# Graph attention kernel: the node stage's five transfers take four consecutive nodes on a partition

## The chip, the cores and the metric

One core of one Trainium2 chip runs the whole program in one launch. The metric is device microseconds of one execution of that program. The kernel before takes 4809.48 us, the median of 3 runs (4803.77 to 4822.28 us).

## What is computed

The graph has 50000 nodes and 50000 edges, sorted by their target node. Node rows are 256 floats wide. Two rounds are computed, each closed by a residual sum and a layer norm:

```python
edge_index = jnp.stack([src, dst])
x = _layernorm(x + gat(x, edge_index, edge_attr_32, lin_W, att_src, att_dst, ...))
x = _layernorm(x + edge_mlp(x, edge_attr_128, src, dst, W0, b0, W1, b1, W2, b2, Wg))
```

The first round is graph attention with 4 heads of 64 and a self loop on every node: per target node a softmax over its edges' logits, then the weighted sum of the sources' projected rows. The second round takes for every edge the rows of its source and target, h = tanh([x_src, x_dst] @ W0 + b0), two further layers, a gate from the edge's 128 attributes, and the mean of the results over the edges of the same source.

## The kernel before

**Stages.** The program is a series of blocks; at the end of each all engines meet. In order of time: weights and keys (to 26 us), a histogram of the target keys (to about 220 us), a rank stage that also projects x and stores it as the table XP (to 1022 us), a message stage in sorted order that writes a table CT of running sums (to 1568 us), a short block that repairs sums across tiles, the **node stage** (1622 to 2698 us), the edge stage (to about 4505 us) and the last layer norm. Edges and nodes are handled in 98 groups of 512, that is G = 4 tiles of P = 128.

**Two orders of the 512 rows of a group.** The helper `tiles(a, g)` (L103) puts row p of tile t on partition p, at place t: a partition holds four rows that lie 128 rows apart in memory, and each is its own run of bytes. The helper `nodes(a, g)` (L107) puts rows 4p to 4p + 3 on partition p: one run four times as long. The rank stage already loads x (L157 in `load_nodes`) and stores XP (L688) by `nodes`.

**The node stage** (L1297 to L1545) makes, for each group g, the row of the first round: the node's last running sum from CT, its own projected row from XP, and x.
- SP (L1329) waits for `n_row` of group g - 2, then loads `n_xp` from XP (528 KB, rows of 1056 bytes) and `n_x` from x (512 KB, rows of 1024 bytes, through `load_rows`, L148).
- POOL (L1336) raises the variance of group g to the power -0.5, then copies four columns of `lastd` into `n_last` (L1340) and issues four indirect gathers of 128 rows of CT for group g + 2 (L1344). Nothing of POOL is queued behind them but the next group's power.
- VectorE (L1428) works in a fixed order: statistics of group g (L1401 to L1408), `exponents` of group g + 1 (L1371 to L1376, of which L1374 needs the gathers), the low halves of group g - 1 (L1419), `shift` (L1413), `row` of group g + 1 (L1381 to L1395). The last operation of `row` releases the loads of group g + 3.
- ScalarE norms the rows (L1492), stores them to `out` (L1497), evacuates the products (L1516) and stores the tables PA (L1521, rows of 1632 bytes) and PB (L1522, rows of 1624 bytes).
- TensorE transposes the normed rows and multiplies them by both halves of W0, each as three products of rounded parts (L1468), 48 matmuls of 406 columns a group.

**Tables that depend on the order.** `lastd` holds for each node the row of CT with its last sum. It is made in the histogram stage in the order of `nodes` (`lastf`, L572) and turned into the order of `tiles` at the end of the rank stage: 16 matmuls with selection matrices `place` (L751 to L755), which POOL fills in the histogram stage (L482 to L488). `rcn` is the reciprocal count of each source; it is counted in the rank stage from two digits of the source key, `LO[1]` and `HI[1]` (L323 to L329), low 7 bits and the rest, which is the order of `tiles`. TensorE's last matmul of that stage (L757) turns the counts of signs into differences, and L819 and L820 make the reciprocal.

Of the kernel before, what the change touches and what calls it, by code (L numbers as in the profile page):

```python
# [21 lines left out]
P = 128  # L22
G = 4
# [33 lines left out]
def gnn_kernel(nc, x, src, dst, e128, e32, lin_W, att_src, att_dst, lin_edge_W, att_edge, bias,  # L57
# [105 lines left out]
    with top:  # L163
# [52 lines left out]
        ki = [alloc(srt, f"key_digit{q}", [P, NT], i32) for q in range(5)]  # L216
# [5 lines left out]
        KEYS_READY = 13  # L222
        ph = ExitStack()
        with ph:
# [6 lines left out]
            with nc.Block(no_gpsimd_drain=True) as block:  # L231
# [67 lines left out]
                def _(dve):  # L299
# [23 lines left out]
                    c.did(nc.vector.tensor_scalar(ki[1][:], KI[:, 1, 0:NT], P - 1, None, ALU.bitwise_and))  # L323
                    c.did(nc.vector.tensor_scalar(ki[3][:], KI[:, 1, 0:NT], 7, None, ALU.arith_shift_right))
# [4 lines left out]
                    c.did(nc.vector.tensor_scalar(HI[1][:], ki[3][:], -0.5, None, ALU.add))  # L329
# [38 lines left out]
        with srt:  # L368
# [4 lines left out]
            place = alloc(srt, "place", [P, G * G, P])  # L373
# [66 lines left out]
            with ph:  # L440
# [15 lines left out]
                with nc.Block(no_gpsimd_drain=True) as block:  # L456
# [15 lines left out]
                    @block.gpsimd  # L472
                    def _(pool):
                        nc.gpsimd.memset(far[:], -BIG).then_inc(h_pad, 1)
                        pool.wait_ge(h_pad, 3)
                        nc.gpsimd.memset(far[:].rearrange("p (r w) -> p r w", w=DW)[:, :, DW - 1:DW], 0.0).then_inc(h_pad, 1)
                        nc.gpsimd.memset(steps[:], 0.0).then_inc(h_pad, 1)
                        for n, (base, fill) in enumerate(((0, 1.0), (1, -1.0), (1 - P, 1.0))):
                            pool.wait_ge(h_pad, 5 + n)
                            nc.gpsimd.affine_select(out=steps[:], in_=steps[:], compare_op=ALU.not_equal, fill=fill,  # L480
                                                    base=base, pattern=[[-1, P]], channel_multiplier=1).then_inc(h_pad, 1)
                        nc.gpsimd.memset(place[:], 0.0).then_inc(h_pad, 1)  # L482
                        pool.wait_ge(h_pad, 9)
                        for r in range(G):
                            for k in range(G):
                                nc.gpsimd.affine_select(out=place[:, r * G + k, :], in_=place[:, r * G + k, :],
                                                        compare_op=ALU.not_equal, fill=1.0, base=k - r * P,
                                                        pattern=[[-1, P]], channel_multiplier=G).then_inc(h_pad, 1)  # L488
# [111 lines left out]
            with ph:  # L600
# [3 lines left out]
                LB = B[3]  # L604
# [13 lines left out]
                with nc.Block(no_gpsimd_drain=True) as block:  # L618
# [81 lines left out]
                    def _(pe):  # L700
# [46 lines left out]
                        pe.wait_ge(r_ot, GROUPS)  # L747
                        pe.wait_ge(h_pad, 9 + G * G)
                        by_quad = lastf[:].rearrange("p (g t) -> p g t", t=G)
                        by_tile = LB[:, 0:NT].rearrange("p (g t) -> p g t", t=G)  # L750
# [9 lines left out]
                    def _(dve):  # L760
# [65 lines left out]
        with ph:  # L826
# [36 lines left out]
            with nc.Block(no_gpsimd_drain=True) as block:  # L863
# [34 lines left out]
                def _(dve):  # L898
# [5 lines left out]
                    dve.wait_ge(h_pad, 10 + G * G)  # L904
# [393 lines left out]
        with ph:  # L1298
# [27 lines left out]
            with nc.Block(no_gpsimd_drain=True) as block:  # L1326
                @block.sync
                def _(sp):
                    def body(g, s, i, last):  # L1329
                        need(sp, n_row, g - 1)  # L1330
                        sp.dma_start(xpn[s][:], tiles(XP, g)).then_inc(n_ld[s], 16)
                        load_rows(sp, xin[s], x, g, last, n_x[s])
# [32 lines left out]
                def _(dve):  # L1365
# [12 lines left out]
                    def row(g, s, i, last):  # L1378
# [12 lines left out]
                        dve.wait_ge(n_x[s], 16 * (i + 1) + 16 * last)  # L1391
# [36 lines left out]
                    def body(g, s, i, last):  # L1428
# [8 lines left out]
                        if not late(g, 1):  # L1437
                            row(g + 1, 1 - s, i if s == 0 else i + 1, late(g, 2))
# [3 lines left out]
                    row(0, 0, 0, False)  # L1442
# [40 lines left out]
                def _(act):  # L1483
# [4 lines left out]
                    def norm(g, s, i, last):  # L1488
# [10 lines left out]
                        act.dma_start(tiles(out, g, TAIL_TILES), x1[s][:, 0:TAIL_TILES, :]).then_inc(x1_st[s], 16)  # L1499
                        act.dma_start(out[N - TAIL_ROWS:N, :], x1[s][0:TAIL_ROWS, TAIL_TILES, :]).then_inc(x1_st[s], 16)  # L1500
# [40 lines left out]
                    act.wait_ge(x1_st[0], 16 * PAIRS)  # L1541
                    act.wait_ge(x1_st[1], 16 * PAIRS + 16)
                    for s in range(2):
                        act.wait_ge(pa_st[s], 16 * PAIRS)
# [505 lines left out]
```

## Time and profile before

| | us |
|---|---|
| median of 3 runs | 4809.48 |
| lowest, highest | 4803.77, 4822.28 |
| span of the profiled execution | 4813.1 |
| node stage, first DMA issue to the next stage's | 1621.8 to 2698.0 |

| engine | busy us | share of the span |
|---|---|---|
| TensorE | 3972.5 | 83% |
| VectorE | 3729.6 | 77% |
| ScalarE | 3089.0 | 64% |
| GpSimd | 2981.9 | 62% |

HBM is read for 567.01 MB and written for 431.82 MB. Of 717533 DMA packets 591298 are under 2 KB. Three queues carry them: q0 is GpSimd's indirect transfers (software), q1 is issued by SyncE and q10 by ScalarE (hardware). Their packets took 30.3%, 19.8% and 21.6% of the 16 engines' time over the whole span.

How to read it: the shares are means over stages that differ. The stage of the change has to be read by itself, in windows of time. A group of 512 nodes in it is one period of every engine, and the question is which wait in a period ends last. The time in which a queue's packets were moved is given as a share of 16 DMA engines; a share times 16 times the length of the window, divided by the bytes, is the engine time of a megabyte. Packets of one engine may overlap, so a share can be a little over 100%.

### The profile page before, as it was taken

The numbers are of one execution on the slowest core, as the hardware profiler recorded it, in microseconds if no ns is written. First come the engines' busy times: TensorE is split into PE (matmuls) and PEld (weight loads), VectorE is DVE, ScalarE is ACT, GpSimd is POOL, SyncE is SP. The second block draws the span as 40 slices with busy tenths as digits, with TensorE's granted clock in tenths as the row PEclk, the third lists the DMA queues.
The fourth block names the chain that finished last, engine by engine and source line by source line (L and its number), as shares of the span: only waits on it lengthen the run. The fifth ranks groups of instructions, "written<-read, shape, count | busy, mean of one in ns | idle before, by whom it ended". The sixth has DMA issues, their size and how long they took to land. (4 is left out here: it accounts for less than half of the span.)

```text
span 4813.1 us, 84225 instructions
## 1 busy us (share of the span) xinstructions
PE 3972.5 (83%) x23546; PEld 3291.7 (68%) x23546; DVE 3729.6 (77%) x11631; ACT 3089.0 (64%) x7157; POOL 2981.9 (62%) x2765
## 2 busy tenths in 40 slices
PE   5899999977777499999999799999999999999200
PEld 3466666655555399999999687777788778777200
DVE  6899999978888699898989476666666666666564
ACT  6866666645555266666666477776777767776575
POOL 1055556567777355555555377777777778777322
PEclk9999999988999699999999899999999999999655
DMA  4255554558666499999999577766767766766696
GB/s 105 51 171 169 168 171 167 169 148 212 199 201 202 151 360 364 349 365 353 365 359 362 175 152 154 153 149 153 152 150 153 154 152 149 153 150 152 218 394 261
DMA packets 717533, 1002.80 MB, mean 208 GB/s; under 512 B 186862, under 2 KB 591298, under 8 KB 704182
## 3 DMA queue, kind: packets, MB, share of 16 engines
q0 software_dynamic: 160768, 323.45, 30.3%
q10 hardware_dynamic: 245565, 375.01, 21.6%
q1 hardware_dynamic: 310861, 300.30, 19.8%
q8 instruction: 154, 2.52, 0.2%
q14 instruction: 185, 1.52, 0.1%
HBM read 567.01 MB, written 431.82 MB: 208 GB/s over the span
## 5 line engine op out<-in xcount | busy, mean ns | idle before, releaser
L1468 PE MATMUL bank<-w0r,n_x1T 128*128 128x406 f32 x4704 | 903.3, 351 | 41.1 <-ACT n_pa L1516 38.9
L1468 PEld LDWEIGHTS bank<-w0r,n_x1T 128*128 128x128 f32 x4704 | 868.0, 189 | 65.6 <-ACT n_pa L1516 63.4
L1612 POOL DMA_INDIRECT out_x<-u_sums,u_row x392 | 635.8, 1622 | 144.4 <-issue 117.1
L1664 PE MATMUL bank<-u_h,w1r 128*108 128x512 f32 (+1 forms) x2646 | 692.4, 407 | 0.0
L635 POOL DMA_INDIRECT DS<-payload,rank_int x392 | 378.2, 965 | 477.0 <-DVE rank_int L810 386.5
L1344 POOL DMA_INDIRECT n_cg<-CT,n_last x392 | 452.0, 1153 | 174.4 <-issue 95.2
L1664 PEld LDWEIGHTS bank<-u_h,w1r 128*108 128x108 f32 (+1 forms) x2646 | 444.5, 175 | 129.8
L1595 POOL DMA_INDIRECT u_pa<-PA,key_int x392 | 388.2, 990 | 167.2 <-issue 120.1
L891 POOL DMA_INDIRECT xg<-XP,ds x392 | 412.4, 1052 | 125.9 <-issue 121.3
L1664 PE MATMUL bank<-w2r,u_h 108*128 108x256 f32 x3528 | 479.2, 280 | 0.0
L427 PE MATMUL bank<-wst,xT 128*128 128x264 f32 x1568 | 421.3, 391 | 51.0 <-DVE xps L436 50.8
L1595 POOL DMA_INDIRECT u_pb<-PB,key_int x392 | 384.2, 980 | 119.5 <-issue 119.5
L1664 PEld LDWEIGHTS bank<-w2r,u_h 108*128 108x128 f32 x3528 | 444.1, 188 | 0.1
L1826 DVE TENSOR_TENSOR u_pb<-u_pb,u_pa 128x512 f32<-128x512 f32 x294 | 198.0, 701 | 265.7 <-DMA u_pb<-PB,key_int 265.7
L427 PEld LDWEIGHTS bank<-wst,xT 128*128 128x128 f32 x1568 | 283.2, 190 | 132.3 <-issue 84.3
L1652 PE MATMUL bank<-ident,u_pb 128*128 128x128 f32 (+1 forms) x1568 | 244.7, 279 | 143.4 <-DVE u_pb L1826 124.0
L1652 PEld LDWEIGHTS bank<-ident,u_pb 128*128 128x128 f32 (+1 forms) x1568 | 176.6, 137 | 234.6 <-DVE u_pb L1826 140.1
L1774 ACT CAST u_msg<-u_message 128x256 fp32r<-128x256 f32 x392 | 158.2, 404 | 263.3 <-DVE u_message L1886 263.3
L1768 ACT ACTIVATE u_gate<-bank,u_rc 128x256 f32<-128x256 f32 x392 | 188.1, 480 | 174.4 <-PE bank L1664 174.2
L1351 POOL TENSOR_TENSOR n_rstd<-n_var,n_half 128x4 f32<-128x4 f32 x98 | 103.8, 1059 | 299.5 <-DVE n_var L1408 299.5
L2018 ACT ACTIVATE f_y<-f_y,f_shift,f_rstd 128x256 f32<-128x256 f32 x392 | 197.9, 587 | 107.0 <-DVE f_shift L1994 103.2
L1751 ACT ACTIVATE bank<-bank,b0s 128x512 f32<-128x512 f32 (+1 forms) x392 | 262.5, 670 | 0.0
(319 smaller groups left out, 10080.4 us busy)
## 6 DMA issues: line engine op xcount, KB each, us to landing
PA<-n_pa ACTq DMA_DIRECT2D x98, 816.0 KB
PB<-n_pb ACTq DMA_DIRECT2D x98, 812.0 KB
XP<-xps ACTq DMA_DIRECT2D x98, 528.0 KB
CT<-ct ACTq DMA_DIRECT2D x98, 528.0 KB
n_xp<-XP SPq DMA_DIRECT2D x98, 528.0 KB
xin<-in_x SPq DMA_DIRECT2D x97, 512.0 KB
n_x<-in_x SPq DMA_DIRECT2D x97, 512.0 KB, 9.8
out_x<-n_x ACTq DMA_DIRECT2D x97, 512.0 KB, 5.0
```

Of the source, the lines that this page charges most:

```text
L427: o = nc.tensor.matmul(acc[:, 0:XW], xT[k][:, h, j * P:(j + 1) * P], wst[:, h, :], start=(h == 0), stop=(h == 1))
L635: pool.indirect_dma_start(out=DS, out_offset=bass.IndirectOffsetOnAxis(ap=ri[s][:, j:j + 1], axis=0), in_=PD[:, g * G + j, :], in_offset=N ...
L891: pool.indirect_dma_start(out=xg[r][:, j, :], out_offset=None, in_=XP, in_offset=bass.IndirectOffsetOnAxis(ap=ds[:, g * G + j, 1:2].bitcas ...
L1344: pool.indirect_dma_start(out=cg[s][:, j, :], out_offset=None, in_=CT, in_offset=bass.IndirectOffsetOnAxis(ap=il[s][:, j:j + 1], axis=0)). ...
L1468: o = nc.tensor.matmul(acc, xT[s][p][:, k, e], w0r[q][:, 2 * half + k, :], start=(n == 0), stop=(n == len(terms) - 1))
L1595: pool.indirect_dma_start(out=buf[s][:, j, 0:w], out_offset=None, in_=table, in_offset=bass.IndirectOffsetOnAxis(ap=KI[:, 1 - q, g * G + j ...
L1612: pool.indirect_dma_start(out=out, out_offset=bass.IndirectOffsetOnAxis(ap=si[s][:, j:j + 1], axis=0), in_=yo[s][:, j, :], in_offset=None, ...
L1652: o = nc.tensor.transpose(TB[k % 2][0:n, j * P:(j + 1) * P], pb[s][:, j, a:a + n], ident[:])
L1664: o = nc.tensor.matmul(acc, a[p], b[q], start=(start and n == 0), stop=(stop and n == 2))
L1751: nc.scalar.activation(TB[k % 2][0:n, :], TB[k % 2][0:n, :], ACT.Tanh, bias=b0s[0:n, k:k + 1])\
L1826: nc.vector.tensor_tensor(pb[s][:, :, a], pb[s][:, :, a], pa[s][:, :, a], ALU.add).then_inc(v_sum, 1)
L2018: o = nc.scalar.activation(y[k][:, j, :], y[k][:, j, :], ACT.Identity, bias=nm[s][:, j:j + 1], scale=rs[s][:, j:j + 1])
```

## The change

Five transfers of the node stage take the order of `nodes` instead of `tiles`: the loads of XP and x, the stores of `out`, PA and PB. The tables in memory keep their layout; what changes is which node sits on which partition between load and store. The last group's x and `out` become one transfer of 84 partitions instead of two. The gathers read the same 512 rows of CT, each of the four now every fourth node. The source key is split into three digits so that the counts come in the order of `nodes`, and `lastd` is a plain copy of `lastf`; the selection matrices and their matmuls go.

```diff
-                    c.did(nc.vector.tensor_scalar(ki[1][:], KI[:, 1, 0:NT], P - 1, None, ALU.bitwise_and))
-                    c.did(nc.vector.tensor_scalar(ki[3][:], KI[:, 1, 0:NT], 7, None, ALU.arith_shift_right))
+                    c.did(nc.vector.tensor_scalar(ki[1][:], KI[:, 1, 0:NT], 2, P - 1, ALU.arith_shift_right,
+                                                  ALU.bitwise_and))
+                    c.did(nc.vector.tensor_scalar(ki[3][:], KI[:, 1, 0:NT], 9, 2, ALU.arith_shift_right,
+                                                  ALU.logical_shift_left))
+                    c.did(nc.vector.tensor_scalar(ki[5][:], KI[:, 1, 0:NT], G - 1, None, ALU.bitwise_and))
...
-                    c.did(nc.vector.tensor_scalar(HI[1][:], ki[3][:], -0.5, None, ALU.add))
+                    c.did(nc.vector.scalar_tensor_tensor(HI[1][:], ki[3][:], -0.5, ki[5][:], ALU.add, ALU.add))
...
-                        nc.gpsimd.memset(place[:], 0.0).then_inc(h_pad, 1)
-                        pool.wait_ge(h_pad, 9)
-                        for r in range(G):
-                            for k in range(G):
-                                nc.gpsimd.affine_select(out=place[:, r * G + k, :], ...)
...
-                        for r in range(G):
-                            for k in range(G):
-                                o = nc.tensor.matmul(by_tile[:, :, r], place[:, r * G + k, :], by_quad[:, :, k],
-                                                     start=(k == 0), stop=(k == G - 1))
-                        o.then_inc(r_tk, 1)
...
+                        nc.vector.tensor_copy(lastd[:], lastf[:])
                         dve.wait_ge(r_tk, 2)
-                        nc.vector.tensor_copy(lastd[:], LB[:, 0:NT])
-                        dve.wait_ge(r_tk, 3)
...
-                        sp.dma_start(xpn[s][:], tiles(XP, g)).then_inc(n_ld[s], 16)
-                        load_rows(sp, xin[s], x, g, last, n_x[s])
+                        sp.dma_start(xpn[s][:], nodes(XP, g)).then_inc(n_ld[s], 16)
+                        load_nodes(sp, xin[s], x, g, last, n_x[s])
...
-                            act.dma_start(tiles(out, g), x1[s][:]).then_inc(x1_st[s], 16)
+                            act.dma_start(nodes(out, g), x1[s][:]).then_inc(x1_st[s], 16)
...
-                        act.dma_start(tiles(PA, g), pa[s][:]).then_inc(pa_st[s], 16)
-                        act.dma_start(tiles(PB, g), pb[s][:]).then_inc(pb_st[s], 16)
+                        act.dma_start(nodes(PA, g), pa[s][:]).then_inc(pa_st[s], 16)
+                        act.dma_start(nodes(PB, g), pb[s][:]).then_inc(pb_st[s], 16)
```

## Rows read from the trace of the kernel before

**Rows 1.** Stretches: busy us (count) of PE, PEld, DVE, ACT, POOL, clock, DMA, GB/s.

```profile
1700.00:2600.00 900.00, 861.07 (x4775) 833.50 (x4773) 811.32 (x2213) 563.63 (x1280) 498.80 (x513) 1.00 1.05 360
4520.00:4740.00 220.00, 0.00 (x0) 0.00 (x0) 150.02 (x749) 169.27 (x336) 68.76 (x42) 0.50 0.99 387
```

**Rows 2.** Waits, 1700 to 2600 us: us in total, times, longest.

```profile
PEld bank L1468 <- ACT n_pa L1516: 58.8, 88, 4.3
DVE n_max L1374 <- DMA n_cg<-CT,n_last: 47.1, 67, 6.2
```

**Rows 3.** Timeline of one period: start us, us, engine, line, operation, idle before.

```profile
2006.02 1.92 POOL L1344 DMA_INDIRECT n_cg<-CT,n_last  x1 [0.31 <-issue]
...
2009.50 0.95 POOL L1344 DMA_INDIRECT n_cg<-CT,n_last  x1 [0.30 <-issue]
2009.53 1.23 DVE L1395 TENSOR_TENSOR n_row<-n_row,n_x 128x1024 f32<-128x1024 f32 x1
...
2010.18 0.38 ACTq L1521 DMA_DIRECT2D PA<-n_pa  x1
...
2010.72 0.40 ACTq L1522 DMA_DIRECT2D PB<-n_pb  x1
...
2014.27 0.18 DVE L1374 TENSOR_TENSOR n_max<-n_self,n_cg 128x16 f32<-128x16 f32 x1 [1.01 <-DMA n_cg<-CT,n_last]
```

**Rows 4.** Timeline, VectorE, a period without a wait.

```profile
2640.92 1.22 DVE L1395 TENSOR_TENSOR n_row<-n_row,n_x 128x1024 f32<-128x1024 f32 x1
...
2651.03 1.23 DVE L1395 TENSOR_TENSOR n_row<-n_row,n_x 128x1024 f32<-128x1024 f32 x1
```

**Rows 5.** Line L1344, landings: issued 1630 to 1633, at 2009.5, at 1922.5.

```profile
DMA to landing us min/median/max: 2.8/2.8/2.9
...
DMA to landing us min/median/max: 4.7/4.7/4.7
...
DMA to landing us min/median/max: 8.8/8.8/8.8
```

**Rows 6.** Queues, 1624.9 to 1626.9, then 2003 to 2004.5: packets, MB, share.

```profile
q1 hardware_dynamic: 742, 0.74, 108.3%
...
q10 hardware_dynamic: 369, 0.59, 106.1%
```

**Rows 7.** Queues in 2006.6 to 2008.6 us, all that moved.

```profile
q1 hardware_dynamic: 427, 0.43, 65.1%
q10 hardware_dynamic: 197, 0.30, 42.3%
```

**Rows 8.** Rank stage, timeline: a scatter that POOL issues beside longer runs.

```profile
702.00 0.96 POOL L635 DMA_INDIRECT DS<-payload,rank_int  x1 [0.31 <-issue]
```

**Rows 9.** Rank stage, queues: 703.9 to 705.4, 705.4 to 706.5, 707.6 to 708.8.

```profile
q1 hardware_dynamic: 160, 0.50, 87.9%
...
q0 software_dynamic: 64, 0.01, 5.8%
...
q10 hardware_dynamic: 108, 0.46, 94.5%
```

**Rows 10.** Timeline of three block ends: weights, rank stage, and the node stage's start.

```profile
24.11 0.90 DVE L338 COPY wst<-bank 128x256 f32<-128x256 f32 x4 [0.41 <-PE bank L363]
...
1012.21 5.76 PE L753 MATMUL bank<-last_by_quad,place 128*128 128x98 f32 x32
...
1018.12 0.99 POOL L640 DMA_INDIRECT DS<-r_s_dst,head_rows  x1 [0.30 <-issue]
...
1019.27 2.60 DVE L820 RECIPROCAL rcn<-found 128x392 f32<-128x392 f32 x1
...
1022.28 0.06 DVE L900 MEMSET first_keys<- 128x4 f32 x1 [0.40 <-PEq L618]
...
1619.35 0.90 POOL L1176 DMA_INDIRECT CT<-heads,z_head_rows  x1 [0.30 <-issue]
1621.75 0.39 SPq L1331 DMA_DIRECT2D n_xp<-XP  x1
```

More of the change, by code:

```diff
@@ L215, in gnn_kernel @@
         krf = [alloc(srt, f"key_rowsf{q}", [P, NC, P]) for q in range(2)]
-        ki = [alloc(srt, f"key_digit{q}", [P, NT], i32) for q in range(5)]
+        ki = [alloc(srt, f"key_digit{q}", [P, NT], i32) for q in range(6)]
         h_pad, h_loaded, h_rows, h_psum, h_chain = (sem("h_pad"), sem("h_loaded"), sem("h_rows"), sem("h_psum"),
@@ L221, in gnn_kernel @@
         KEYS = 16 * (2 * len(loads) + 2)
-        KEYS_READY = 13
+        KEYS_READY = 14
         ph = ExitStack()
@@ L481, in _ @@
                                                     base=base, pattern=[[-1, P]], channel_multiplier=1).then_inc(h_pad, 1)
-                        nc.gpsimd.memset(place[:], 0.0).then_inc(h_pad, 1)
-                        pool.wait_ge(h_pad, 9)
-                        for r in range(G):
-                            for k in range(G):
-                                nc.gpsimd.affine_select(out=place[:, r * G + k, :], in_=place[:, r * G + k, :],
-                                                        compare_op=ALU.not_equal, fill=1.0, base=k - r * P,
-                                                        pattern=[[-1, P]], channel_multiplier=G).then_inc(h_pad, 1)
                     @block.tensor
@@ L746, in _ @@
                         count_src(GROUPS - 1, 1, True)
[L747 to L750, printed above, removed]
-                        for r in range(G):
-                            for k in range(G):
-                                o = nc.tensor.matmul(by_tile[:, :, r], place[:, r * G + k, :], by_quad[:, :, k],
-                                                     start=(k == 0), stop=(k == G - 1))
-                        o.then_inc(r_tk, 1)
+                        pe.wait_ge(h_pad, 8)
                         pe.wait_ge(r_keys, 2)
@@ L903, in _ @@
                         c.did(nc.vector.memset(ks[s][:], 0.0))
-                    dve.wait_ge(h_pad, 10 + G * G)
+                    dve.wait_ge(h_pad, 9)
                     c.did(nc.vector.tensor_scalar(pk[0][:], pn[:], 2, G - 1, ALU.arith_shift_right, ALU.bitwise_and))
@@ L1376, in exponents, with row @@
                         nc.vector.tensor_tensor(ea[s][:, 1], sf[s][:], mx[s][:], ALU.subtract).then_inc(n_exl, 1)
-                    def row(g, s, i, last):
+                    def row(g, s, i):
                         cr.at(g * 7)
@@ L1390, in row @@
                                                           ALU.mult))
-                        dve.wait_ge(n_x[s], 16 * (i + 1) + 16 * last)
+                        dve.wait_ge(n_x[s], 16 * (i + 1))
                         cr.wait()
@@ L1437, in body @@
                         if not late(g, 1):
-                            row(g + 1, 1 - s, i if s == 0 else i + 1, late(g, 2))
+                            row(g + 1, 1 - s, i if s == 0 else i + 1)
                     for s in range(2):
@@ L1441, in _ @@
                     exponents(0, 0, 0)
-                    row(0, 0, 0, False)
+                    row(0, 0, 0)
                     looped(dve, body)
@@ L1496, in norm @@
                         if not last:
-                            act.dma_start(tiles(out, g), x1[s][:]).then_inc(x1_st[s], 16)
+                            act.dma_start(nodes(out, g), x1[s][:]).then_inc(x1_st[s], 16)
                             return
-                        act.dma_start(tiles(out, g, TAIL_TILES), x1[s][:, 0:TAIL_TILES, :]).then_inc(x1_st[s], 16)
-                        act.dma_start(out[N - TAIL_ROWS:N, :], x1[s][0:TAIL_ROWS, TAIL_TILES, :]).then_inc(x1_st[s], 16)
+                        act.dma_start(out[(GROUPS - 1) * G * P:N, :].rearrange("(p t) w -> p t w", t=G),
+                                      x1[s][0:TAIL_QUADS]).then_inc(x1_st[s], 16)
                     def high(g, s):
@@ L1540, in _ @@
                         tables(GROUPS - 2 + s, s)
-                    act.wait_ge(x1_st[0], 16 * PAIRS)
-                    act.wait_ge(x1_st[1], 16 * PAIRS + 16)
                     for s in range(2):
+                        act.wait_ge(x1_st[s], 16 * PAIRS)
                         act.wait_ge(pa_st[s], 16 * PAIRS)
```

2 lines of the change are left out of this document (removed).

## Prediction

> **What bounds the kernel now.** The windows come first. In the node stage the queues carry 360 GB/s, TensorE is busy 96% of the time and VectorE 90%, all at full clock [rows 1]; the reader is to see that three resources are nearly full at once, so busy shares alone don't say which one ends a group. The last stage shows that more can be moved: 387 GB/s, with runs of 8 KB [rows 1].
>
> The waits say which. Between 1700 and 2600 us VectorE has one wait of weight, L1374 for the gathers of CT, 47.1 us in 67 of 85 groups, the longest 6.2; TensorE's weight loads wait 58.8 us, but for ScalarE, which evacuates only after the norm, which waits for VectorE [rows 2]. TensorE's wait is the same wait passed on. A period without it is 10.11 us, the step between two rows of VectorE [rows 4]; 900 us for 85 groups are 10.6. So the stage runs at VectorE's chain of 10.11 us plus 0.5 for the gathers. I take 10.11 as the floor: nothing in the change touches an operation of VectorE, ScalarE or TensorE in the loop.
>
> The timeline gives the loop. POOL issues the last of four gathers at 2009.50, it lands 4.7 us later, and VectorE waited 1.01 us for it at 2014.27 [rows 3, 5]. Landing 3.7 us after issue would have cost nothing. With no other traffic a gather lands in 2.8 [rows 5]. What is issued for group g + 2 hangs on the variance of group g, so one late landing lengthens two periods once: a microsecond less at landing takes about 49 us off the stage, until the waits are gone.
>
> **What the change does, part by part.**
>
> The gains of the packets. Engine time of a megabyte is share x 16 x window / MB. Runs of 1 KB loaded alone: 1.083 x 32 / 0.74 = 46.8 us; tables of 1.6 KB stored alone: 1.061 x 24 / 0.59 = 43.2 [rows 6]. The rank stage has the longer runs already: its loads of 4 KB and 2 KB take 0.879 x 24 / 0.50 = 42.2, its stores of 4.2 KB 0.945 x 19.2 / 0.46 = 39.4 [rows 9]. A group has 1.07 MB of loads, 1.67 of tables and 0.52 of `out`, so the change saves 1.07 x 4.6 + 1.67 x 3.8 + 0.52 x 7.4 = 15.1 engine us, over 16 engines 0.94 us a period of DMA time. None of it is on the path by itself. It shortens what lies in front of the gathers.
>
> How much of it the last gather gets is the unknown. From 2006.6 to 2008.6 only q1 and q10 moved packets [rows 7], while a gather issued before, and from 2006.02 on a second [rows 3], were pending: the gathers don't take a turn, they come after hardware work that is already queued. The same is seen with longer runs: a scatter issued at 702.00 [rows 8] moves nothing until 705.4, while q1 moves the x load and the keys, and its packets come right behind them [rows 9]. So the excess of the last gather over the idle case, 4.7 - 2.8 = 1.9 us, is work in front of it. If only that work shrinks by the tenth that packets save, the landing gains 0.2 us; if the backlog ends earlier by the whole 0.94, it gains 0.9. The middle is 0.5: 49 x 0.5 = 25 us. The bounds are 10 us and the ordinary waits in full: 47.1 less three waits of 5 to 6 us, the longest 6.2 [rows 2], is 30 in 85 groups, and about 35 in the stage. I take 25. The longest goes with a gather that took 8.8 us to land [rows 5]; such waits stand some 300 us apart, so their cause is not the ordinary backlog, and I leave them in.
>
> The start of the stage: 2.1 MB of loads stand ahead of the first gathers, 4.6 engine us a megabyte less are 0.6 us; bounds 0 and 2.
>
> End of the rank stage: 32 matmuls of 5.76 us go [rows 10]. They are on TensorE between the counts and L757, and the reciprocal of 2.60 us follows; without them VectorE would be done before 1018.5. But POOL's last scatter is issued at 1018.12, and from such an issue to the next block it is 1621.75 - 1619.35 = 2.4 us [rows 10]. So the next block would start at 1020.5 instead of 1022.28: the gain is 1.7 us, not 5.8. What is late next is that scatter.
>
> The keys: one more whole-table operation on VectorE and one with two inputs, together under the 0.90 us of L338, against a wait of 0.41 for TensorE behind them [rows 10]: 0 to 0.5 us lost, taken as 0.2. The selection matrices on POOL lie in a stage in which it has nothing else to do and go free. The copy of `lastf` runs under L757. The gathers' rows, every fourth node: the sorted-order gathers of the message stage read rows at random in the same way, so nothing; bounds -0.1 and +0.2 us a landing, inside the range. The SyncE and ScalarE issues stay five a group, in the same places.
>
> Sum: 25 + 0.6 + 1.7 - 0.2 = 27 us off the span of 4813.1, which is 4786. The profiled execution lies 3.6 us above the median of 4809.48; on the median the same sum gives **4782 us**.
>
> **A rule against the change.** The last stage's 387 GB/s [rows 1] is above what the node stage moves. The Trainium skill (DMA: Bandwidth & Descriptors, Where 436 GB/s comes from) has the HBM side bind at about 358 GB/s for one core of the pair; by that the node stage's 360 would be the limit, longer runs would free nothing and the sum would be 1.5 us. The row of the last stage speaks against it on this core.
>
> **The rivals.**
>
> *Nothing moves in the stage* (it would give 4808 us: 1.5 off). For it: the fixed part of a landing, 2.8 of 4.7 us, is the larger; the next tables are issued at 2010.18 and 2010.72 [rows 3], and a gather that comes in behind the first of them has as many bytes ahead of it as before. Against it: 0.94 us of DMA time must go somewhere. That rows don't join into longer packets ends here too; they do in the rank stage, 0.50 MB in 160 packets [rows 9].
>
> *The gathers fall behind the tables* (slower). [...] Place: the last gather, 0.7 us ahead of PA and 1.2 ahead of PB by issue [rows 3], but slower to start. With PA and PB wholly in front, 1.67 x 39.4 / 16 = 4.1 us, it lands at 6.9, 2.2 us later than now: 49 x 2.2 = 108 us. If that hits half of the groups it is 54 us: 4862. It decides from a landing over 4.7. The gather of 8.8 us [rows 5] shows how long one can be held back. Against it: the order of issue favours the gather, and a wait moves the tables later, not the gather.
>
> *The gathers take turns.* A landing of 2.8 plus a packet of each other queue, under 1 us, is within the 3.7 that cost nothing: the ordinary 35 us go in full, 4809.5 - 35 - 2 = 4772. The two stretches in which q0 stands still speak against it [rows 7, 9]. The Trainium skill (DMA: Bandwidth & Descriptors, Queues, rings and completion order) has each DMA engine go round its queues packet by packet, which is this rival.
>
> **How the numbers follow.** Forecast, 4782, its own range 4766 to 4798: 0.47. Nothing moves, 4798 to 4812: 0.29. Behind the tables, 4815 to 4917: 0.16. Turns, or the three long waits gone as well (down to 4755): 0.08. Half a per cent, about what a measurement of this kernel can tell from no change, is 24 us, so 4785.4 and 4833.5. Of the forecast case some 0.36 lies below the first, 0.11 above it. Faster: 0.36 + 0.08 = 0.44. Same: 0.11 + 0.29 + 0.04 of the slower case = 0.44. Slower: 0.12. The range 4758 to 4838 leaves out most of that last 0.12 and 0.03 below.
>
> **What would show it.** Queues q1 and q10 with about a quarter of their packets in the node stage and 39 to 43 engine us a megabyte. The last gather of a group landing near 4.2 us after issue, L1374's wait between 1700 and the stage's end down from 47 to under 30 us, periods at 10.1 to 10.4, the stage shorter by 20 to 30 us. The node stage's start 1.7 us earlier against the message stage's. Wrong would be: landings over 4.7 with the same q10 packets in front of q0's; periods of 10.11 throughout with landings near 3; or a floor other than VectorE's chain, seen as a wait of TensorE that VectorE didn't cause.

## The result, and the profile after

The changed kernel takes 4840.56 us (median of 4 runs, 4835.11 to 4847.72) against 4812.94 for the kernel before on the same chip. The ratio is 1.0066, 95% interval 1.0044 to 1.0088: 28 us more where 27 us less was forecast. The time lies 2.6 us above the upper end of the range, on the side that the rival *the gathers fall behind the tables* had described.

The profiled execution spans 4837.6 us, 24.5 more than before. The first and the last sum of x and XP in the node stage (columns: start us, us, engine, line, operation) bracket the stage:

```profile
1632.73 1.22 DVE L1378 TENSOR_TENSOR n_x<-n_x,n_xp 128x1024 f32<-128x1024 f32 x1
...
2695.18 1.23 DVE L1378 TENSOR_TENSOR n_x<-n_x,n_xp 128x1024 f32<-128x1024 f32 x1
```

The same two of the kernel before (its L1393):

```profile
1636.29 1.22 DVE L1393 TENSOR_TENSOR n_x<-n_x,n_xp 128x1024 f32<-128x1024 f32 x1
...
2661.64 1.23 DVE L1393 TENSOR_TENSOR n_x<-n_x,n_xp 128x1024 f32<-128x1024 f32 x1
```

Before: 1025.4 us between them; after: 1062.4. The node stage grew by 37 us. The stage began 3.6 us sooner, and what follows it took 2142.4 us and not 2151.5. Neither is the change's doing as far as these traces tell: over the kernels below, all alike behind the node stage, that last part took from 2142 to 2159 us, and the first sum began anywhere from 1623 to 1643.

The window of 1700 to 2600 us, which answers [rows 1] (stretch, us, busy us and count of PE, PEld, DVE, ACT and POOL, clock, DMA share, GB/s):

```profile
1700.00:2600.00 900.00, 839.52 (x4614) 799.82 (x4613) 783.20 (x2145) 543.02 (x1232) 474.62 (x494) 1.00 0.95 348
```

The waits in it, which answer [rows 2] (us, times, longest):

```profile
DVE n_max L1359 <- DMA n_cg<-CT,n_last: 72.7, 45, 2.9
PEld bank L1453 <- ACT n_pa L1501: 59.4, 98, 1.2
```

Its queues and issues (packets, MB, share; then issues, KB each, median us to landing):

```profile
q10 hardware_dynamic: 35674, 180.99, 52.5%
q1 hardware_dynamic: 23617, 87.34, 24.4%
q0 software_dynamic: 15846, 44.64, 18.6%
...
PA<-n_pa ACTq DMA_DIRECT2D x82, 816.0 KB, 5.0
...
out_x<-n_x ACTq DMA_DIRECT2D x82, 512.0 KB, 3.5
n_cg<-CT,n_last POOLq DMA_INDIRECT x328, 4.7
```

Queues and issues of the kernel before in the same stretch:

```profile
q10 hardware_dynamic: 134718, 186.39, 58.5%
q1 hardware_dynamic: 90437, 91.20, 30.3%
q0 software_dynamic: 16343, 46.07, 16.1%
...
out_x<-n_x ACTq DMA_DIRECT2D x86, 512.0 KB, 5.0
...
n_cg<-CT,n_last POOLq DMA_INDIRECT x343, 5.1
```

What to see there. The packets did join, in number to about a quarter, and the queues are less busy: DMA share 0.95 for 1.05. Yet less is moved, 348 GB/s for 360, since VectorE waits longer for the gathers: 72.7 us for 47.1. It waits less often, 45 times for 67, so each wait is longer. And the median gather lands sooner than before, 4.7 us for 5.1. A median hides the one gather in four that counts. The timeline of two groups shows it:

```profile
2006.02 0.94 POOL L1329 DMA_INDIRECT n_cg<-CT,n_last  x1 [0.30 <-issue]
...
2006.59 0.34 ACTq L1506 DMA_DIRECT2D PA<-n_pa  x1
2007.09 0.34 ACTq L1507 DMA_DIRECT2D PB<-n_pb  x1
...
2011.23 0.17 DVE L1359 TENSOR_TENSOR n_max<-n_self,n_cg 128x16 f32<-128x16 f32 x1 [1.44 <-DMA n_cg<-CT,n_last]
...
2016.17 0.95 POOL L1329 DMA_INDIRECT n_cg<-CT,n_last  x1 [0.30 <-issue]
...
2018.08 0.34 ACTq L1506 DMA_DIRECT2D PA<-n_pa  x1
...
2021.31 0.18 DVE L1359 TENSOR_TENSOR n_max<-n_self,n_cg 128x16 f32<-128x16 f32 x1
```

In the first group the last gather is issued 0.57 us ahead of PA, and VectorE waits 1.44 us. In the next it is issued 1.91 us ahead of PA, and nobody waits. Then it is 0.56 again, and the wait is 2.58 us. So it goes on, every second group. As I read it, the late tables are the work of the wait itself: VectorE's delay passes on through TensorE to the evacuation and so to the issue of PA, not to the gather, which was issued before. The next group is thereby rid of the tables, runs without a wait, and the one after meets them again.

From the trace's records of single packets I worked out the following for the last gather of each group (78 groups from the middle of the stage; medians). 'Gap' is the time from its issue to PA's, 'end' the end of its last packet after its issue, 'ahead' the bytes of PA and PB whose packets started before that packet, 'over 0.4' the share of its packets that took longer than 0.4 us; in the kernel before half of the gathers' packets take 0.16 to 0.19. How many groups count as behind 600 KB shifts by a few with the way of counting; that it is half of them in six kernels and few in the others does not.

```
kernel            ratio   PA starts*  groups with >600 KB ahead   their gap, end, over 0.4        the others'
before            1       2.58        6 of 78                     -                                0.68, 3.73, 12%
changed           1.0066  1.46        41 of 78                    0.57, 4.93,  7%                  1.92, 3.87, 28%
loads as rows e3  1.0065  1.44        41                          0.56, 4.89,  3%                  1.92, 3.68, 27%
f6 tables + out   1.0088  1.40        39                          0.56, 4.85,  2%                  1.92, 3.74, 25%
e8                1.0081  1.39        39                          0.56, 4.83,  3%                  1.92, 3.80, 23%
g1                1.0064  1.38        39                          0.56, 4.55,  1%                  1.92, 3.62, 24%
e6 out as rows    1.0023  2.15        12                          -                                0.87, 3.79, 18%
f2 tables         1.0023  2.29        9                           -                                0.70, 3.67, 19%
f3 out            0.9993  2.49        7                           -                                0.64, 3.59, 15%
f4 loads + tables 1.0024  2.23        9                           -                                0.70, 3.62, 18%
f5 loads + out    0.9991  2.55        6                           -                                0.65, 3.51, 21%
f1 loads          0.9988  2.56        7                           -                                0.68, 3.50, 23%
e1 all as rows    1.0082  2.67        7                           -                                2.03, 4.85,  7%
e2 tables as rows 1.0081  2.69        8                           -                                1.79, 4.75, 20%
* a tenth of PA's packets started, us after PA's issue, median
```

The experiments are told in the order in which they ran; this table is the short of them.

### The profile page after: what moved, and what is told of

Same layout as the page of the kernel before. It is cut to its first block and busy times, and to the rows that moved or that the text cites. A ratio compares the mean times of both kernels' runs of the same rounds, so it can differ in the third digit from the quotient of the medians.

```text
span 4837.6 us, 84127 instructions
## 1 busy us (share of the span) xinstructions
PE 3970.6 (82%) x23514; PEld 3277.1 (68%) x23514; DVE 3726.8 (77%) x11632; ACT 3086.0 (64%) x7157; POOL 2964.3 (61%) x2748
```

## The experiments

The first guess was the length of the tables' packets (Theory A), with the order of the gathered rows as its rival.

**e1_rows.** All five transfers in the new order, but in packets of one row.

```diff
-            pa = [alloc(ph, f"n_pa{s}", [P, G, AW]) for s in range(2)]
+            pa = [alloc(ph, f"n_pa{s}", [P, G, AW + 8])[:, :, 0:AW] for s in range(2)]
```
and so for n_x, n_xp, n_x1 and pb.

> Edit: the changed kernel with 8 floats of padding behind each tile row of n_x, n_xp, n_x1, pa and pb, so that every packet of the five transfers is one row again (1.0 or 1.6 KB) while the order of the nodes, of the digits and of the gathered rows stays that of the change. Theory A (the long packets of the tables in front of the last gather of every second group cost the 28 us): the time goes back to that of the kernel before, 4813 within 0.4%, ratio to before 0.997 to 1.003; the waits for n_cg in the node stage fall from 72.7 us in 900 to about 47. Theory B (the new order itself, each gather reading every fourth row of its table, is slower to fetch): the time stays at 4841, ratio 1.005 or more, and waits for n_cg stay at about 73 us.

Measured: 4841.54 us, ratio 1.0082 (1.0060 to 1.0104). Theory A said 0.997 to 1.003. The waits are of another kind than the changed kernel's, 72 of 1.06 us on the mean and not 45 of 1.6:

```profile
DVE n_max L1359 <- DMA n_cg<-CT,n_last: 76.0, 72, 4.2
```

**e2_tables_rows.** Only pa and pb padded.

> Edit: the changed kernel, but only pa and pb padded, so the tables leave in packets of one row (1.6 KB) and the loads and out stay at 4 KB or more. Theory A (the tables' long packets): the 28 us go, and with them some of the transfer time that the loads' and out's longer packets save shows as a gain: ratio to before 0.990 to 1.000, a last landing at or under 4.7 us in every group. Theory C (the loads' long packets, which come due with the last gather of the other groups): the time stays within 0.3% of 4841 (ratio 1.004 to 1.008).

Measured: 4843.46 us, ratio 1.0081 (1.0060 to 1.0103). A miss for Theory A as well, and just beyond Theory C's 1.008.

**e3_loads_rows.** Only n_x and n_xp padded.

> Edit: the changed kernel, but only n_x and n_xp padded, so the loads go row by row and the tables and out keep their long packets. Theory A (tables): ratio to before 1.004 to 1.012, the strict alternation of one group with a wait for n_cg of 1.2 to 2.6 us and one without stays. Theory C (loads): ratio 0.998 to 1.002, the alternation is gone.

Measured: 4835.13 us, ratio 1.0065 (1.0044 to 1.0086), in Theory A's range and with its alternation; Theory C is out. The loads' length changes nothing.

**e4_gather_early.** POOL issues the sources' copy and the first gather ahead of power.

```diff
                     def body(g, s, i, last):
+                        if not late(g, 2):
+                            gather_first(g + 2, s)
                         power(g, s)
                         if not late(g, 2):
-                            gather(g + 2, s)
+                            gather_rows(s, range(FIRST, G))
```

> Edit: the changed kernel, but the sources' copy and the first of a group's four gathers are issued by GpSimd ahead of its power instruction and not behind it, so the last gather is issued some 1 us sooner. If the last landing is what VectorE waits for, the wait for n_cg of 1.2 to 2.6 us in every second group shrinks by about 1 us: 49 such groups, 49 us of 4841, ratio to before 0.994 to 0.999. If power is then late enough to hold up ScalarE or VectorE instead, or the gather meets the same tables sooner, nothing is gained: ratio 1.004 to 1.008 or more.

Measured: 4764.48 us, ratio 0.9911 (0.9884 to 0.9937), more than was expected of a microsecond: the waits go altogether (4.9 us in 900). POOL had stood idle between the last gather and the variance; the first gather now uses that time, and the last one is issued 3.3 us ahead of PA and not 0.6 (timelines at h1 below).

Lengths being no simple cause, the next four asked for the order.

**e7_gather_quads.** The kernel before, with the gathered rows alone in the new order.

```diff
-                        nc.vector.tensor_copy(lastd[:], LB[:, 0:NT])
+                        nc.vector.tensor_copy(lastd[:], lastf[:])
```

> Edit: the kernel before, all five transfers in its own tile order, but the table of last rows taken without reordering (the copy reads lastf), so each gather fetches the rows of every fourth node, as in the changed kernel. The output then belongs to mixed-up nodes; the work is the same. In the kernel before 6 to 12 in 100 packets of the middle gathers took over 0.4 us and 2 in 100 of the last; in the changed kernel, with packets of either length, 13 to 27 in 100 of some gathers. Theory B1 (the order of the gathered rows makes the packets slow): ratio to before 1.005 to 1.009, waits for n_cg near 75 us in 900, mean gather packet near 250 ns. Theory B2 (the order of the rows in the five transfers, whose reads and writes of memory run beside the gather, makes them slow): ratio 0.998 to 1.002, mean gather packet near 208 ns.

Measured: 4800.8 us, ratio 0.9996 (0.9980 to 1.0011). (By place, first to last gather of a group, 2, 3, 9 and 12 in 100 packets of the kernel before take over 0.4 us; the expectation had put the low share at the last.)

**e8_gather_tiles.** The changed kernel, with `place`, its matmuls and the copy from LB put back.

> Edit: the changed kernel with the reordering of the table of last rows put back (place, its sixteen matmuls and the copy from LB), so the five transfers move four consecutive nodes a partition while each gather fetches 128 consecutive nodes' rows. The output then belongs to mixed-up nodes. Theory B1 (order of the gathered rows): the gather's packets are as quick as before, and what is left is the transfers' saved time: ratio to before 0.990 to 1.001, waits for n_cg 20 to 47 us in 900. Theory B2 (order of the transfers): ratio 1.005 to 1.009, waits near 75 us, mean gather packet near 250 ns.

Measured: 4841.55 us, ratio 1.0081 (1.0064 to 1.0098). Both ways round the order of the gathered rows is cleared; Theory B1 is out.

**e5_before_early.** The edit of e4 on the kernel before.

> Edit: the kernel before, with the sources' copy and the first of a group's four gathers issued by GpSimd ahead of power and not behind it, as in e4_gather_early. There the wait for n_cg fell to 4.9 us in 900 and VectorE's chain of 10.09 us a group was all that was left. Theory D (with the gather early, VectorE's chain bounds the node stage in either order of nodes, and the change itself is worth nothing): ratio to before 0.989 to 0.994, within 0.3% of e4_gather_early. Theory E (the changed order then still brings its saved transfer time): this kernel is slower than e4_gather_early by over 0.3%, ratio to before 0.995 or more.

Measured: 4770.34 us, ratio 0.9937 (0.9921 to 0.9954). Theory D in its ratio, 0.26% behind e4's; h1 and h2, timed side by side, settle what that is.

**e6_out_rows.** The changed kernel with n_x1 alone padded.

> Edit: the changed kernel with only n_x1 padded, so that out leaves in packets of one row (1 KB), the rest as changed. out's packets run beside the first gathers' in the trace. If the length of out's packets holds up the gather (the last variant of Theory A, after the loads and the tables were ruled out one at a time): ratio to before 0.998 to 1.002. If packet length has nothing to do with it: 1.005 to 1.009, as for all five padded together (1.0082).

Measured: 4813.93 us, ratio 1.0023 (1.0008 to 1.0037), just above the first range. Most of the loss is gone with `out` in rows, and it is there with everything in rows. So lengths matter, but by which meets which.

That asked for one kind of transfer at a time, in the kernel before, with the change's order and packets, and for the gather's own memory.

**f1_loads**, **f2_tables**, **f3_out**: `tiles` to `nodes` in the two loads, in PA and PB, in `out`.

```diff
-                        act.dma_start(tiles(PA, g), pa[s][:]).then_inc(pa_st[s], 16)
+                        act.dma_start(nodes(PA, g), pa[s][:]).then_inc(pa_st[s], 16)
```

> Edit: the kernel before with the change's order and packets in the two loads alone (XP and x, 4 KB packets); table of last rows, tables and out stay in tile order. The output then belongs to mixed-up nodes; the work is the same. The order of the gathered rows being no cause, one of the three kinds of transfers has to be, or they only do it together. If the loads do it: ratio to before 1.005 to 1.009, over 12 in 100 gather packets above 0.4 us (6 in 100 before). If they don't: 0.994 to 1.002, the saved transfer time at most.

Measured: 4800.36 us, ratio 0.9988 (0.9974 to 1.0001).

> Edit: the kernel before with the change's order and packets in the stores of PA and PB alone (6.5 KB packets). The rows of the tables then stand in mixed-up places; the work is the same. If the tables do it: ratio to before 1.005 to 1.009 and over 12 in 100 gather packets above 0.4 us. If they don't: 0.994 to 1.002.

Measured: 4807.92 us, ratio 1.0023 (1.0008 to 1.0039).

> Edit: the kernel before with the change's order and packets in the store of out alone (4 KB packets); the rows of the output stand in mixed-up places. Its packets lie around the first three gathers in the trace, and padding it alone in the changed kernel took the ratio from 1.007 to 1.002. If out does it: ratio 1.004 to 1.009 and over 12 in 100 gather packets above 0.4 us. If not: 0.994 to 1.002.

Measured: 4801.91 us, ratio 0.9993 (0.9980 to 1.0007). No one does it alone; the tables alone cost 0.23%, a little more than their "if they don't" of 1.002, the other two nothing. The share of gather packets over 0.4 us rose to 10 in 100 with the loads and 11 with the tables, from 6, and cost next to nothing: slow packets are not what the time hangs on.

**g1_spread.** 128 copies of the row of nodes without an edge.

```diff
-                    pool.dma_start(CT[NP:NP + 1, :], dummy[:]).then_inc(z_st, 16)
+                    pool.dma_start(CT[NP:NP + P, :], dummy[:]).then_inc(z_st, 16)
...
-                        nc.vector.tensor_copy(lastd[:], lastf[:])
+                        c.step(nc.vector.tensor_scalar(spread[:], lastf[:], float(NP), pf[:, 0:1], ALU.is_equal, ALU.mult))
+                        nc.vector.tensor_tensor(lastd[:], spread[:], lastf[:], ALU.add)
```

> Edit: the changed kernel with 128 copies of the row of zeros that nodes without an edge gather (row NP of CT), and each partition taking its own copy; the answer is the same. Destinations are drawn at random, 50,000 for 50,000 nodes, so by an estimate 37 in 100 nodes have no edge and all of them fetch the one row, some 47 reads of it in each gather of 128. Theory H (packets of a gather that several engines fetch at once stand in line for that one row; the new order only makes them meet more often): gather packets over 0.4 us fall from 14 in 100 to under 3, waits for n_cg in 900 us from 73 to under 15, ratio to before 0.988 to 0.996. Theory B2 (the order of the transfers' rows disturbs the gather in the memory wherever it reads): little moves, ratio 1.003 to 1.009. The extra instructions at the end of the rank stage cost about 1.5 us in either.

Measured: 4834.28 us, ratio 1.0064 (1.0040 to 1.0087); 13 in 100 packets over 0.4 us. Theory H is out.

**f4_loads_tables**, **f5_loads_out**, **f6_tables_out**: the edits of f1 to f3, two at a time.

> Edit: the kernel before with the change's order and packets in the loads and in the tables, out and the table of last rows in tile order; the output belongs to mixed-up nodes, the work is the same. Loads alone took the packets over 0.4 us from 6 to 10 in 100, tables alone to 11, out left them at 6; all three gave 14. Theory S (loads and tables each slow the gather's packets, and their shares add up until the last gather is late in every second group): ratio to before 1.003 to 1.009, waits for n_cg over 60 us in 900. Theory V (it takes out with them, since with out alone back to packets of a row the changed kernel stood at 1.002): 0.999 to 1.0025.

Measured: 4813.91 us, ratio 1.0024 (1.0008 to 1.0040): Theory V, and no more than with the tables alone.

> Edit: the kernel before with the change's order and packets in the loads and in out; tables and last rows in tile order; the output belongs to mixed-up nodes, the work is the same. Theory S (loads and tables are the pair): 0.996 to 1.001, some 10 in 100 gather packets over 0.4 us. Theory V1 (out with the loads is the pair): 1.004 to 1.009.

Measured: 4801.5 us, ratio 0.9991 (0.9978 to 1.0004). Theory V1 is out.

> Edit: the kernel before with the change's order and packets in the tables and in out, both on ScalarE's queue; loads and last rows in tile order; rows of the tables and the output stand in mixed-up places, the work is the same. Theory S: 1.000 to 1.003, as with the tables alone (1.0023). Theory V2 (out with the tables is the pair: ScalarE's whole queue in long packets beside the gather): 1.004 to 1.009 and waits for n_cg near 73 us in 900.

Measured: 4850.06 us, ratio 1.0088 (1.0057 to 1.0120). Theory V2: tables with `out` are the pair. The wait for n_cg in 1700 to 2600 us is 49.3 us with the tables alone (f2), 41.5 with `out` alone (f3), and with both (f6):

```profile
DVE n_max L1374 <- DMA n_cg<-CT,n_last: 68.1, 44, 2.3
```

The issues of the same stretch (median us to landing last), of f2, of f3 and of f6:

```profile
PA<-n_pa ACTq DMA_DIRECT2D x85, 816.0 KB, 5.0
...
out_x<-n_x ACTq DMA_DIRECT2D x85, 512.0 KB, 3.9
```

```profile
PA<-n_pa ACTq DMA_DIRECT2D x86, 816.0 KB, 6.0
...
out_x<-n_x ACTq DMA_DIRECT2D x86, 512.0 KB, 4.8
```

```profile
PA<-n_pa ACTq DMA_DIRECT2D x83, 816.0 KB, 4.7
...
out_x<-n_x ACTq DMA_DIRECT2D x83, 512.0 KB, 3.5
```

`out`, PA and PB go down one queue in this order. With both in long packets `out` has landed 3.5 us after its issue for 5.0 before, its last packet ends 0.95 us after PA's issue for 2.13, and a tenth of PA's packets has started 1.40 us after PA's issue. With either in rows it is 2.15 to 2.55. It isn't the early end of `out` that lets PA go: with `out` in rows it ends as early (0.94 us after PA's issue in e6, 1.00 in f4, 1.10 in f2), and PA's first packet still starts at 1.7 to 1.8 and not at 1.0; in h1, below, PA starts at 1.0 while `out` ends at 1.6. The last gather moves its packets 2.5 to 4.9 us after its issue, so with a gap of 0.6 to PA it used to be nearly through when the tables began (0.6 + 2.6 = 3.2 us after its issue, by an estimate from the table), and now it isn't (0.6 + 1.4 = 2.0, ahead of its first packet). In the table above the kernels with PA at 1.4 are those with half of their groups behind 600 KB of tables.

**h3_tables_late.** PA and PB behind the cast into n_x1T.

```diff
                             high(g - 1, 1 - s)
+                        if not early(g, 3):
+                            tables(g - 3, 1 - s)
...
-                            tables(g - 2, s)
```

> Edit: the changed kernel with PA and PB issued by ScalarE one instruction later, behind the cast into n_x1T of the next group (some 2.4 us later) and not ahead of it; order and packets as in the change. Theory W (the tables, let loose early by a quick out, get in front of the last gather): the last gather is through before they start, waits for n_cg in 900 us fall from 73 to under 30, ratio to before 0.989 to 0.999. Theory X (the order of tables and out makes the gather's reads slow in the memory, whenever they meet): the waits stay at 60 or more, ratio 1.003 to 1.009. If the tables now meet the first gathers of the next group instead, or their landing holds up the evacuation two groups later, waits move there and the ratio is over 1.000 with fewer waits for n_cg.

Measured: 4836.51 us, ratio 1.0063 (1.0045 to 1.0080). By the letter this is Theory X's number, the wait for n_cg (68.4 us in 900) too, but the edit missed: the timeline shows that ScalarE's cast had been waiting for nothing and now runs at once, so the tables leave at the same place, 2.32 us after `out` and 0.56 after the last gather.

```profile
2002.33 0.34 ACTq L1482 DMA_DIRECT2D out_x<-n_x  x1
...
2004.09 0.94 POOL L1329 DMA_INDIRECT n_cg<-CT,n_last  x1 [0.30 <-issue]
2004.33 0.64 ACT L1491 CAST n_x1T<-bank 128x512 fp32r<-128x512 f32 x1
2004.65 0.34 ACTq L1506 DMA_DIRECT2D PA<-n_pa  x1
```

It tells nothing between W and X. What it does show is that an operation ahead of the tables on ScalarE moves nothing when TensorE has its operand ready: the trace of the changed kernel had the cast 1.35 us behind PA's issue, and I had read that place as fixed.

**h1_after_early** and **h2_before_early**: e4 and e5 side by side.

> Edit: none against e4_gather_early (the changed kernel, first gather ahead of power); it is timed again to stand side by side with h2_before_early. The change's own worth with the gather early: theory D (VectorE's chain of 10.1 us a group is all that is left in either): ratio to before 0.989 to 0.994 and within 0.2% of h2_before_early; theory E (its shorter transfers still bring something): below h2_before_early by over 0.2%.

> Edit: none against e5_before_early (the kernel before, first gather ahead of power), timed again in one call with h1_after_early. Theory D: ratio to before 0.990 to 0.995, the two within 0.2% of each other, h1 some 1 to 2 us ahead for the rank stage's shorter end. Theory E: over 0.2% behind h1.

Measured: 4761.89 us, ratio 0.9905 (0.9883 to 0.9927), and 4764.57 us, ratio 0.9910 (0.9890 to 0.9931). They are 0.06% apart: Theory D (h1 is 2.7 us ahead, where 1 to 2 were expected). The window of 1700 to 2600 us, the wait in it and two lines of the timeline, of h1:

```profile
1700.00:2600.00 900.00, 891.51 (x4974) 866.24 (x4973) 843.85 (x2309) 586.44 (x1332) 470.24 (x533) 1.00 1.01 375
```

```profile
DVE n_max L1366 <- DMA n_cg<-CT,n_last: 4.2, 3, 1.5
```

```profile
2014.18 1.16 POOL L1332 DMA_INDIRECT n_cg<-CT,n_last  x1 [0.30 <-issue]
...
2017.49 0.34 ACTq L1513 DMA_DIRECT2D PA<-n_pa  x1
```

Window, wait and gathers' landing of h2:

```profile
1700.00:2600.00 900.00, 889.33 (x4965) 864.69 (x4964) 842.43 (x2303) 585.50 (x1329) 474.54 (x531) 1.00 1.06 374
```

```profile
DVE n_max L1381 <- DMA n_cg<-CT,n_last: 6.9, 13, 1.0
```

```profile
n_cg<-CT,n_last POOLq DMA_INDIRECT x354, 6.4
```

The last gather is issued 3.31 us ahead of PA, in its own time, and 89 groups go through in 900 us for 83. With `out` and the tables in packets as long as in the changed kernel, and PA's as quick to start (a tenth of them 1.3 us after its issue), h1 has no wait: the order and the packets do no harm where the gather isn't in their way. This is the best evidence for Theory W, if not a trial of it alone, since the gather is also issued earlier against VectorE's need. In h2 a gather takes 6.4 us to land, more than the 5.8 of e1, the longest among the slower kernels, and almost nobody waits. h1 beats both kernels of the case by 46 us and more.

## Why the prediction was wrong, point by point

**The bound was right.** VectorE's chain of 10.11 us a group and the wait for the last gather make the stage. Its length follows the wait for n_cg in 900 us: 982 us with 4.2 (h1), 1025 with 47.1 (before), 1039 with 56.3 (e6), 1054 with 68.1 (f6), 1062 with 72.7 (changed). With the waits gone a group takes 10.09 to 10.10 us (h1). TensorE was never the bound.

**The transfer term was right in its sum, by luck in its parts.** Engine time of a megabyte in 1700 to 2600 us, share x 14,400 / MB: loads 47.8 before and 40.2 after, ScalarE's queue 45.2 and 41.8. A group saves 1.07 x 7.6 + 2.19 x 3.4 = 15.6 engine us; the forecast had 15.1. But the loads saved 8.1 where 4.9 stood, and ScalarE's queue 7.5 where 10.2 stood, `out` before having been priced by a load's row; the two errors cancel. A third of the saving was paid back where no term stood: the gathers' megabyte went from 50.3 to 60.0 engine us, 0.53 MB x 9.7 = 5.2 us a group.

**The step that failed is the next one**: that the saved 0.94 us "shortens what lies in front of the gathers", worth 0.2 to 0.9 us of the last gather's landing, -25 us in the sum. The first three gathers did get it: their first packets start 3.51, 2.66 and 2.39 us after issue, for 4.34, 3.78 and 3.03 before (medians of the 78 groups). The last one got 0.1 us, 2.47 for 2.58; gathers that ran alone at 1630 to 1633 us needed 1.65. What moved with it were the tables behind it, which the sum had nowhere: they start 1.1 us sooner (2.58 to 1.46 after PA's issue), between the last gather's own packets. In half of the groups the last gather's end rose from 3.73 to 4.93 us, in the other half it is 3.87.

**The rival had the mechanism, at too low a chance.** *The gathers fall behind the tables* named place, direction and the half of the groups, with 54 us; measured were 28 by the medians and 37 in the stage. Its size: I had the whole 1.67 MB in front of the gather. In the late groups of the changed kernel it was some 0.98 MB, worked in between the gather's own packets, and the landing was 1.2 us later and not 2.2. At the forecast's 49 us for a microsecond that would be 59 us, or 29 halved as the rival halved it; the stage grew by 37, so the price was of the right order. In two us of such a group both queues move, as the answer for 2008 to 2010 us shows:

```profile
q10 hardware_dynamic: 87, 0.57, 68.7%
q0 software_dynamic: 45, 0.11, 21.6%
```

What I held against it was "the order of issue favours the gather, and a wait moves the tables later, not the gather". The first half is worth 0.57 us of issue against the 2.5 us from the last gather's issue to its first packet. The second half is right, and it is why every second group, not every one, is late. The chance of 0.16 should have been nearer to the forecast's own: [rows 3] had the gap of 0.7 us, and [rows 7] a gather that stands still while the other queues move. Long packets in the tables alone don't bring it about: the ratio is 1.0023 (f2).

**The turns.** In those two us 87 packets of tables and 45 of gathers went side by side, so here the gather does share. The rival that gathers take turns had priced that as harmless, under 1 us over the idle 2.8; the last packet ends at 4.93.

**The rank stage.** POOL's last scatter is late next, as said: the next block starts 2.69 us after it and not 4.16, so 1.5 us gained for 1.7 forecast. The answer to [rows 10]:

```profile
1017.82 0.99 POOL L634 DMA_INDIRECT DS<-r_s_dst,head_rows  x1 [0.30 <-issue]
...
1020.51 0.06 DVE L885 MEMSET first_keys<- 128x4 f32 x1 [2.79 <-PEq L612]
```

**The keys.** The copy of `wst` starts at 24.38 for 24.11 [rows 10], 0.27 us lost for 0.2 forecast:

```profile
24.38 0.90 DVE L341 COPY wst<-bank 128x256 f32<-128x256 f32 x4
```

**The start of the node stage**, 0.6 us forecast, can't be told in a scatter of 20 us. **The gathered rows**, taken as nothing: right, 0.9996 alone. **The long waits** of 5 to 6 us, left in, are gone in the changed kernel (longest 2.9) and come back in others (5.4 in e3, otherwise alike); their cause is open.

**The rule on the memory side.** The node stage moves 375 GB/s in h1 and 374 in h2 over 900 us. The Trainium skill (DMA: Bandwidth & Descriptors, Where 436 GB/s comes from) puts the HBM side at about 358 for one core; these windows of one core that runs alone speak against it as the last stage's had, and the measurement decides.

**What stays open.** Theory W rests on the pair, on the traces and on h1; a delay of the tables alone was meant and not achieved. Why PA starts sooner only when both are long isn't explained, `out`'s end being no reason (f2, f4, e6). And e1 and e2 are slow by another way: PA starts late, few groups are behind 600 KB, and still the last gather ends at 4.85 and 4.75 us in nearly all groups, for 3.73. The gathers' megabyte takes 61 and 68 engine us in them, for 50 before (queue rows of 1700 to 2600 us, e1 and then e2):

```profile
q0 software_dynamic: 15753, 44.37, 18.9%
q0 software_dynamic: 15744, 44.36, 20.9%
```

e2 and f5 have packets of the same lengths in all five transfers and differ in the order of the tables' rows (and of the gathered rows, which e7 and e8 clear): 1.0081 for 0.9991. So the new order with tables in rows costs as much as the whole change, and how is open; that some of the changed kernel's loss comes from the order as well (Theory X) isn't ruled out. What is shown is that the length of `out`'s packets, order kept, is worth most of it (e6), and that an earlier gather takes all of it.

## What to carry to other kernels

Before a transfer is made quicker, look at what stands behind it on its queue, and whether that then meets the transfer on which the bound engine waits. A saving of DMA time is worth only what the last arrival gets of it; here it was worth less than nothing, and two edits that cost 0.23% and nothing alone cost 0.88% together. The cheaper remedy was to issue the awaited gather earlier into idle time of its engine: it took 46 us off, and left nothing of the packets' length to gain or lose.

## What the runs showed of the hardware

Rows of 1 to 1.6 KB that stand together on both sides joined to packets of 4.1 to 6.5 KB, which take 38 to 39 ns a KB of 1000 bytes (medians), for 42 to 45 in rows. Packets of a gather (four rows, 4.2 KB) take 0.16 to 0.19 us in their middle half in the kernel before, and 6 in 100 take over 0.4 us, 15 in 100 in the changed one; the reads of one row shared by over a third of the nodes (an estimate, as in g1's expectation) are not the reason (13 in 100 with 128 copies). Where they fall on groups that have time to spare they cost nothing: in the changed kernel the last gathers of the groups that aren't late have 28 in 100 of them, those of the late ones 7. PA's first packet starts 1.0 us after its issue where `out` and the tables are both in long packets, and 1.7 to 2.0 where either is in rows (2.2 and 2.3 in e5 and h2, where both are in rows and the gather is early).
